# The end of set-up in another order on three engines, and a part of u scaled by GpSimd

## The chip, the cores and the metric

One core of a Trainium2 chip computes the whole problem. The time is device microseconds, the median of several executions. One more execution was taken with the hardware profiler. All times below are from its trace, counted from the first instruction.

## What is computed

The input u has 8 sequences of 1024 positions and 256 channels. The kernel normalises each position over its channels, sends the result through two branches, and adds their product to u:

```python
xn = _layernorm(x, axis=-1)
s = _L0_attn_ref(xn, ...)          # causal filter of 128 taps for each channel, plus xn * D
g = _silu(_L0_ffn_ref(xn, ...))
x = x + s * g
```

`_L0_ffn_ref` is a gated unit, 256 to 704 to 256, whose four operands are rounded to FP4 with one scale for each block of 16 values:

```python
gate = fp4_linear(x, w_gate)
y = fp4_linear(x, w_up)
h = jax.nn.silu(gate) * y
return fp4_linear(h, w_down)
```

The taps of the filter are a real part of a sum of 64 complex exponentials for each channel.

## The kernel before

The 8192 positions are 64 tiles of 128. The gated unit takes two tiles in a step, 32 steps in all (NP). The filter needs the normalised input as fp16 high and low parts in the buffer `xh`, with 16 groups of four tiles.

**Set-up** (to about 91 us) makes the filter's taps `kt`, the statistics of all tiles, and the rounded and transposed weights. Near its end it already treats the first pairs of tiles: `x_norm(p)` on ScalarE (L665) normalises pair p, `x_first` and `x_second` on VectorE (scales at L897 to L902, `inverse` at L930, rounding at L944 and L949) round it, `x_parts` (L957) writes the fp16 parts, `x_transpose` (L1313) and `x_copy` (L672) turn them. `gate_up(m)` (18 matmuls at L1325) makes gate and up of tile m, `silu_gate(m)` (L682) takes SiLU of the gate half, and `h_mult` (L973) multiplies.

**A step** of VectorE first takes the largest of each block (L911, wide TENSOR_REDUCE of 120 blocks), then scales (L914, L918, L922), `inverse` (L930), `h_mult`, rounding (L944 in two pieces, each behind a `square` of ScalarE at L697, then L949), `h_parts` (L981), `x_parts`, and the second `h_mult`. GpSimd makes the tables of scales (`tables`, L515 to L533) between L918 and `h_parts`; VectorE waits for them on `tb_p`. In this order `h_mult` of the next tile opens the way for the next gate_up on TensorE (`h_v`).

**The groups of u** are a third line of work. `a_scale(g)` on ScalarE (L649, four activations of 128x256, normalised with `rs_c` and `nm_c`) is done in place in `gbuf`; `a_high(g)` (L659) writes the fp16 high part; `a_low(g)` on GpSimd (L538) the low part. Each of steps 0 to 7 does the high and low parts of two groups. In steps 4 to 7 a step scales one group (the even one); the odd groups above 5 are the extra ones: before, group 7 in set-up, 9 and 11 in step 1, and 13 and 15 in step 2, all by ScalarE. From step 8 (`S_CONV`) TensorE adds the filter's matmuls (L1358, L1362) to each step, and GpSimd multiplies the branches.

**Order.** Each engine runs the program written for it in line, and they meet in counting semaphores. Nothing is rearranged by a scheduler: what is written first runs first. The taps are scaled on ScalarE (L856, L858: `kt`, `kh`), GpSimd subtracts (`kl`, L587), and SyncE then stores the filter in DRAM (16 DMAs) in step 2 of its own list, between a load of x and a copy of the input to the output. The first `load_t` of the filter is in step 8. Loads of x (L404) wait for `x_r`, which VectorE counts at each L949.

## Time and profile before

| | us |
|---|---|
| median of 3 runs | 572.89 (572.12 to 573.24) |
| the profiled execution | 570.88 |
| its span, first to last instruction | 568.8 |
| VectorE busy | 530.7 (93%) |
| TensorE busy | 477.2 (84%) |
| ScalarE busy | 409.2 (72%) |
| GpSimd busy | 212.0 (37%) |

The busy shares are means over three stretches: set-up to some 91 us, steps 0 to 7 without the filter to some 204 us, and steps 8 to 31 with it. The mean granted clock of TensorE was 0.979. In a timeline a row is one instruction or several of the same kind in a line, with the engine's idle time ahead of it and who ended it in square brackets.

### The profile page before, as it was taken

The numbers are of one execution on the slowest core, as the hardware profiler recorded it, in microseconds if no ns is written. First come the engines' busy times: TensorE is split into PE (matmuls) and PEld (weight loads), VectorE is DVE, ScalarE is ACT, GpSimd is POOL, SyncE is SP. The second block draws the span as 40 slices with busy tenths as digits, with TensorE's granted clock in tenths as the row PEclk, the third lists the DMA queues.
The fourth block names the chain that finished last, engine by engine and source line by source line (L and its number), as shares of the span: only waits on it lengthen the run. The fifth ranks groups of instructions, "written<-read, shape, count | busy, mean of one in ns | idle before, by whom it ended". The sixth has DMA issues, their size and how long they took to land.

```text
span 568.8 us, 13319 instructions
## 1 busy us (share of the span) xinstructions
PE 477.2 (84%) x4981; PEld 332.1 (58%) x4981; DVE 530.7 (93%) x685; ACT 409.2 (72%) x583; POOL 212.0 (37%) x316
## 2 busy tenths in 40 slices
PE   0003474777999999999999999999999999999996
PEld 0000342344555567777777777777777777776675
DVE  6999975898999999999999999999999999999987
ACT  6949758799999976666666666667676666666554
POOL 1499601444555551111111111123233333237770
PEclk9999869889999999999999999999999999999999
DMA  5990002242222135353535353535444353526998
GB/s 162 350 314 1 1 19 93 92 103 94 92 93 94 56 93 165 96 146 100 148 94 167 94 167 93 165 97 145 117 125 135 114 149 112 150 75 124 191 175 177
DMA packets 101954, 70.80 MB, mean 124 GB/s; under 512 B 8864, under 2 KB 101536, under 8 KB 101792
## 3 DMA queue, kind: packets, MB, share of 16 engines
q1 hardware_dynamic: 94624, 62.73, 37.5%
q0 software_dynamic: 7280, 7.34, 8.5%
q8 instruction: 39, 0.64, 0.5%
q14 instruction: 11, 0.09, 0.1%
HBM read 61.28 MB, written 16.12 MB: 136 GB/s over the span
## 4 chain that ended last, share of the span: by engine, by line
PE 63%; DVE 25%; issue 7%; ACT 4%; DMA 0%; SPq 0%; DVEq 0%; ACTq 0%
PE ps L1325 32%; PE ps L1343 10%; PE ps L1345 5%; PE ps L1334 5%; PE ps L1358 4%; PE ps L1362 4%; DVE work L1033 4%; DVE work L949 3%; DVE work L944 3%; DVE work L973 2%; DVE sm L911 2%; PE ps L1313 2%; DVE xh L1011 1%; DVE xh L1001 1%; DVE work L981 1%
## 5 line engine op out<-in xcount | busy, mean ns | idle before, releaser
L1325 PE MATMUL ps<-wgu,work 128*128 128x512 f16 (+1 forms) x1152 | 243.8, 367 | 21.6 <-DVE work L973 20.8
L1325 PEld LDWEIGHTS ps<-wgu,work 128*128 128x128 f16 x1152 | 110.1, 99 | 132.9 <-issue 20.4
L682 ACT ACTIVATE work<-ps,con 128x704 f32<-128x704 f32 x64 | 54.2, 847 | 95.4 <-PE ps L1325 95.4
L1343 PE MATMUL ps<-wdh,work 128*128 128x256 f16 x704 | 87.2, 272 | 0.3 <-ACT work L677 0.2
L677 ACT COPY work<-ps 128x1408 f16<-128x1408 f16 x64 | 84.8, 1325 | 1.6 <-PE ps L1334 1.6
L944 DVE SCALAR_TENSOR_TENSOR work<-work 128x960 f32<-128x960 bf16 (+2 forms) x67 | 72.0, 1112 | 5.0 <-ACT work L697 5.0
L548 POOL TENSOR_TENSOR gbuf<-gbuf,xh 128x256 f32<-128x256 f32 (+1 forms) x42 | 37.8, 929 | 94.0 <-DVE work L957 86.7
L930 DVE TENSOR_TENSOR work<-work,ps 128x960 f32<-128x960 f32 (+2 forms) x67 | 71.5, 1105 | 1.2
L949 DVE SCALAR_TENSOR_TENSOR work<-work 128x1920 f16<-128x1920 bf16 (+3 forms) x36 | 69.7, 1936 | 1.2
L1343 PEld LDWEIGHTS ps<-wdh,work 128*128 128x128 f16 x704 | 65.2, 98 | 7.6 <-ACT work L677 0.4
L911 DVE TENSOR_REDUCE sm<-work 128x120 f32<-128x1920 f32 (+2 forms) x33 | 68.0, 2059 | 1.3
L697 ACT ACTIVATE work<-work 128x960 bf16<-128x960 f32 (+2 forms) x67 | 61.7, 960 | 5.6 <-DVE work L930 5.0
L973 DVE TENSOR_TENSOR work<-work,ps 128x704 f32<-128x704 f32 x64 | 56.4, 881 | 9.0 <-ACT work L682 8.8
L981 DVE TENSOR_TENSOR work<-work,sm 128x1408 f16<-128x1408 f16 (+1 forms) x66 | 54.4, 866 | 5.6 <-DVE work L949 4.2
L515 POOL TENSOR_SCALAR sm<-sm 128x2 int32<-128x2 int32 x32 | 7.6, 239 | 137.6 <-DVE sm L918 137.6
L538 POOL TENSOR_TENSOR xh<-gbuf,xh 128x1024 f16<-128x1024 f32 x16 | 38.8, 2445 | 49.4 <-ACT xh L659 39.4
L686 ACT ACTIVATE gbuf<-ps,sm 128x256 f32 (+1 forms) x64 | 30.2, 473 | 33.0 <-PE ps L1345 32.9
L1334 PE MATMUL ps<-id,work 128*128 128x128 f16 x704 | 49.9, 219 | 3.7 <-DVE work L981 3.6
L1345 PE MATMUL ps<-wdl,work 128*128 128x256 f16 x384 | 52.4, 273 | 0.0
L1358 PE MATMUL ps<-xh,work 128*128 128x64 f16 x768 | 50.3, 192 | 0.0
L1334 PEld LDWEIGHTS ps<-id,work 128*128 128x128 f16 x704 | 43.2, 98 | 11.9 <-DVE work L981 6.0
L1362 PE MATMUL ps<-xh,work 128*128 128x56 f16 x768 | 50.1, 191 | 0.0
(155 smaller groups left out, 682.7 us busy)
## 6 DMA issues: line engine op xcount, KB each, us to landing
work<-kpad SPq DMA_DIRECT2D x64, 512.0 KB, 3.8
gbuf<-u_rev SPq DMA_DIRECT2D x4, 2048.0 KB, 17.9
work<-L_attn_u SPq DMA_DIRECT2D x32, 256.0 KB, 2.9
out<-gbuf POOLq DMA_DIRECT2D x7, 1024.0 KB, 11.5
work<-L_attn_u SPq DMA_DIRECT2D x1, 1024.0 KB, 5.3
out<-gbuf SPq DMA_DIRECT2D x3, 256.0 KB, 2.2
work<-L_ffn_w_down SPq DMA_DIRECT2D x1, 704.0 KB, 7.7
work<-L_ffn_w_gate SPq DMA_DIRECT2D x1, 640.0 KB, 4.6
```

The costliest lines, as they stand in the source:

```text
L677: nc.scalar.copy(hT[par], src).then_inc(hT_a, 1)
L911: own.mark(V.tensor_reduce(bm[:, cols], by_blk[pp][:, cols], AX_X, ALU.max, apply_absolute_value=True))
L930: V.tensor_tensor(v, v, sc, ALU.mult).then_inc(v_v, 1)
L944: own.mark(V.scalar_tensor_tensor(v, d_bf[:, c], C0, v, ALU.add, ALU.subtract))
L949: return V.scalar_tensor_tensor(r_f16[:, c], d_bf[:, c], C0, by_blk[pp][:, c], ALU.add, ALU.subtract)
L973: V.tensor_tensor(vb[par][:, I * t:I * t + I], sg, p_gu[:, I:2 * I], ALU.mult).then_inc(h_v, 1)
L1325: last = T.matmul(p_gu[:, a:b], xT[par][:, t, c, :], wgu[:, part, c % 2, a:b], start=(n == 0), stop=(n == len(todo) - 1))
L1334: last = T.transpose(dst[:, c, :], hilo[par][:, t, c * P:c * P + P], id16[:])
L1343: T.matmul(dst, hT[t][:, c, :], wdh[:, c, :], start=(c == 0), stop=False)
L1345: last = T.matmul(dst, hT[t][:, c, :], wdl[:, c, :], start=False, stop=(c == RT - 1))
L1358: T.matmul(dst, tpl[half][:, 2 * c + tp, 0:P], col[:, xp, :], start=(n == 0), stop=False)
L1362: last = T.matmul(dst1, tpl[half][:, 2 * c + tp, P:2 * P], before, start=False, stop=(n == 2))
```

## The change

The core of the diff:

```diff
@@ GpSimd, end of set-up
-            pool.wait_ge(k_split, 2)
-            nc.gpsimd.tensor_tensor(kl, kt, kh, ALU.subtract).then_inc(k_split, 1)
+            for n, g in enumerate((7, 9, 11)):
+                pool.wait_ge(nm_ok, 2 if n == 0 else 4)
+                if n == 1:
+                    pool.wait_ge(k_free, 1)
+                for t in range(4 * g, 4 * g + 4):
+                    ins = nc.gpsimd.tensor_scalar(gbuf[:, t, :], gbuf[:, t, :], rs_c[:, t:t + 1], nm_c[:, t:t + 1],
+                                                  ALU.mult, ALU.add)
+                ins.then_inc(a_xp, 1)
@@ GpSimd, steps
                 tables(it, it < NP - 2, it >= 1)
+                if it == 1:
+                    pool.wait_ge(k_split, 2)
+                    nc.gpsimd.tensor_tensor(kl, kt, kh, ALU.subtract).then_inc(k_split, 1)
@@ ScalarE
+            input_scales(1)
+            x_norm(2, 0)
+            norm_scales(1)
+            a_scale(13)
             square(-1, 0, True, False, 0)
             act.wait_ge(w_lo, 3)
             act.wait_ge(w_h, 4)
             silu_gate(0)
-            input_scales(1)
-            norm_scales(1)
             weights_out(range(8, 11))
-            x_norm(2, 0)
-            a_scale(7)
+            a_scale(15, 0, 2)
+            square(0, 1, True, False, 0)
+            x_norm(3, 1)
+            silu_gate(1)
+            x_copy(1, 1)
             weights_out(range(11, 13))
+            a_high(0, 2)
+            a_high(1, 2)
+            act.wait_ge(a_xp, 3)
             act.wait_ge(k_sc, 1)
             nc.scalar.activation(kt, kt, ACT.Copy, scale=mxs).then_inc(k_split, 1)
             act.wait_ge(k_split, 1)
             nc.scalar.copy(kh, kt).then_inc(k_split, 1)
-            x_copy(1, 1)
-            for it in range(PEEL):
-                step(it, it % 2, True, it >= 1, True, True, it >= 1, it >= 2, a2=True, td1=it >= 3, first=it >= 1,
-                     more=(None, 9, 13, None)[it])
-                if it in (1, 2):
-                    a_scale(it * 4 + 7)
+            for it in range(1, PEEL):
+                step(it, it % 2, True, True, True, True, True, it >= 2, a2=True, td1=it >= 3, late=it == 1,
+                     more=15 if it == 3 else None)
@@ VectorE
             x_first(1)
+            x_scales()
+            largest(0, 1, True, False)
             largest_of_rows(k_row1, 1, k_one, p_row1)
-            x_scales()
+            h_mult(0, 0, 0)
             x_second(1)
-            h_mult(0, 0, 0)
             x_parts(1, 1)
+            scales(0, True, False)
+            inverse(1, True, False)
@@ TensorE
+            reverse(1)
             pe.wait_ge(w_ca, 8)
             gate_up(0, 0, 0, 1)
-            reverse(1)
+            pe.wait_ge(k_max, 1)
+            T.transpose(p_row1[0:1, :], mxi[:, 3:4], id32).then_inc(k_row1, 1)
...
             gate_up(1, 1, 0, None)
+            pe.wait_ge(con_ok, 1)
+            x_transpose(1, 1)
             pe.wait_ge(w_ca, 9)
             transposed_down(3)
             pe.wait_ge(w_ca, 10)
             transposed_down(4)
-            pe.wait_ge(con_ok, 1)
-            x_transpose(1, 1)
-            pe.wait_ge(w_ca, 13)
```

Step 0 is no longer a step of its own: its pieces are written into set-up on ScalarE and VectorE. VectorE's function `scales_and_largest` is split into `largest` and `scales`. In step 1 `a_scale(2)` of ScalarE comes after `x_norm(4)` (`late`), and step 3 does the second half of group 15 (`more`). The number of groups that `a_high` waits for is adapted. Line numbers of the changed kernel are higher: by 1 in GpSimd's first part, by 10 or 11 in most of ScalarE, by 15 to 22 on VectorE, by 26 to 31 on TensorE.

VectorE before, from the end of `x_first(1)` to the inverse of step 0 (L936, L938 are x_scales; L1039, L1041 largest_of_rows; L1075 to L1163 the powers of the filter's largest):

```order
L930 TENSOR_TENSOR work<-work,ps 128x512
L1039 TENSOR_REDUCE ps<-ps 1x1
L1041 COPY work<-ps 1x128
L936 TENSOR_SCALAR sm<-ps 128x64
L938 SCALAR_TENSOR_TENSOR sm<-ps,sm 128x64
L944 SCALAR_TENSOR_TENSOR work<-work 128x512
L949 SCALAR_TENSOR_TENSOR work<-work 128x512
L973 TENSOR_TENSOR work<-work,ps 128x704
L957 TENSOR_TENSOR work<-work,sm 128x2x256 x2
L1075 TENSOR_SCALAR ps<-ps 128x1
L1077 TENSOR_SCALAR ps<-ps 128x1
L1080 RECIPROCAL ps<-ps 128x1
```
VectorE now, the same stretch (L955, L957 are x_scales; L1058, L1060 largest_of_rows; L992 is h_mult; L976 x_parts):

```order
L955 TENSOR_SCALAR sm<-ps 128x64
L957 SCALAR_TENSOR_TENSOR sm<-ps,sm 128x64
L926 TENSOR_REDUCE sm<-work 128x32
L1058 TENSOR_REDUCE ps<-ps 1x1
L1060 COPY work<-ps 1x128
L992 TENSOR_TENSOR work<-work,ps 128x704
L963 SCALAR_TENSOR_TENSOR work<-work 128x512
L968 SCALAR_TENSOR_TENSOR work<-work 128x512
L976 TENSOR_TENSOR work<-work,sm 128x2x256 x2
L933 SCALAR_TENSOR_TENSOR sm<-sm,ps 128x32
L941 RECIPROCAL ps<-sm 128x32
L949 TENSOR_TENSOR work<-work,ps 128x512
```
The largest, the scales and the inverse of step 0 now stand ahead of the powers, and `h_mult` stands ahead of the rounding.

ScalarE before, from `silu_gate(0)` (L697 ahead of it is square(-1)) to `silu_gate(1)`; L649 is the scaling of group 7, L856 and L858 are the taps:

```order
L665 ACTIVATE work<-work,nmr,rstd 128x256 x2
L649 ACTIVATE gbuf<-gbuf,sm 128x256 x4
L812 COPY wdl<-ps 128x1024
L812 COPY wdl<-ps 128x512
L856 ACTIVATE work<-work 128x256
L858 CAST work<-work 128x256
L672 COPY work<-ps 128x1024
L697 ACTIVATE work<-work 128x512
L665 ACTIVATE work<-work,nmr,rstd 128x256 x2
L659 ACTIVATE xh<-gbuf 128x4x128x2
L682 ACTIVATE work<-ps,con 128x704
```
ScalarE now, from square(-1) (L708) to the taps (L874, L876); L659 is half of group 15, L693 are the two SiLU, L670 both high parts:

```order
L822 COPY wdh<-ps 128x1024 x2
L822 COPY wdh<-ps 128x768
L659 ACTIVATE gbuf<-gbuf,sm 128x256 x2
L708 ACTIVATE work<-work 128x512
L676 ACTIVATE work<-work,nmr,rstd 128x256 x2
L693 ACTIVATE work<-ps,con 128x704
L683 COPY work<-ps 128x1024
L822 COPY wdl<-ps 128x1024
L822 COPY wdl<-ps 128x512
L670 ACTIVATE xh<-gbuf 128x4x128x2 x2
L874 ACTIVATE work<-work 128x256
```
The square of step 0 (L708) and `silu_gate(1)` now stand ahead of the last two copies of weights, the taps behind the high parts of groups 0 and 1.

GpSimd before, from the memset that ends its work on the weights to the tables of step 1:

```order
L585 MEMSET xh 128x2x64
L587 TENSOR_TENSOR work<-work 128x256
L517 TENSOR_SCALAR sm<-sm 128x32
L528 CAST sm<-sm 128x64
L530 TENSOR_TENSOR sm<-sm 128x64
L538 TENSOR_TENSOR xh<-gbuf,xh 128x4x128x2 x2
L515 TENSOR_SCALAR sm<-sm 128x2
```
GpSimd now, the same stretch and the tables of step 1:

```order
L586 MEMSET xh 128x2x64
L592 TENSOR_SCALAR gbuf<-gbuf,sm 128x256 x12
L518 TENSOR_SCALAR sm<-sm 128x32
L529 CAST sm<-sm 128x64
L531 TENSOR_TENSOR sm<-sm 128x64
L539 TENSOR_TENSOR xh<-gbuf,xh 128x4x128x2 x2
L516 TENSOR_SCALAR sm<-sm 128x2
```
The subtraction of the taps (L587) has gone behind the tables of step 1, and twelve scalings of `gbuf` stand in its place.

## Rows read from the trace of the kernel before

**Rows 1.** Busy tenths of VectorE in 40 slices of the span (the page).

```profile
DVE  6999975898999999999999999999999999999987
```

**Rows 2.** Timeline, VectorE, end of set-up: start us, us, engine line, [idle before <-releaser].

```profile
85.97 0.29 DVE L1039 TENSOR_REDUCE ps<-ps 1x1 f32<-1x128 f32 x1 [3.30 <-PE ps L1409]
...
91.74 0.69 DVE L930 TENSOR_TENSOR work<-work,ps 128x512 f32<-128x512 f32 x1
...
97.18 0.69 DVE L944 SCALAR_TENSOR_TENSOR work<-work 128x512 f32<-128x512 bf16 x1 [4.75 <-ACT work L697]
...
100.83 2.15 DVE L911 TENSOR_REDUCE sm<-work 128x120 f32<-128x1920 f32 x1
```

**Rows 3.** Timeline, VectorE, steps 1 to 5.

```profile
107.58 0.89 DVE L973 TENSOR_TENSOR work<-work,ps 128x704 f32<-128x704 f32 x1 [0.93 <-ACT work L682]
...
116.24 2.15 DVE L911 TENSOR_REDUCE sm<-work 128x120 f32<-128x1920 f32 x1
...
130.78 2.15 DVE L911 TENSOR_REDUCE sm<-work 128x120 f32<-128x1920 f32 x1
...
138.14 0.89 DVE L973 TENSOR_TENSOR work<-work,ps 128x704 f32<-128x704 f32 x1 [1.54 <-ACT work L682]
...
146.74 2.15 DVE L911 TENSOR_REDUCE sm<-work 128x120 f32<-128x1920 f32 x1
...
155.52 2.16 DVE L949 SCALAR_TENSOR_TENSOR work<-work 128x1920 f16<-128x1920 bf16 x1
...
161.08 2.15 DVE L911 TENSOR_REDUCE sm<-work 128x120 f32<-128x1920 f32 x1
```

**Rows 4.** Timeline, ScalarE, end of set-up and one later step.

```profile
82.77 0.63 ACT L697 ACTIVATE work<-work 128x512 bf16<-128x512 f32 x1 [4.16 <-DVE work L930]
...
93.36 1.50 ACT L812 COPY wdl<-ps 128x1024 f16<-128x1024 f16 x2 [2.32 <-PE ps L1300]
...
98.03 1.07 ACT L659 ACTIVATE xh<-gbuf 128x1024 f16<-128x1024 f32 x1
...
157.18 0.85 ACT L682 ACTIVATE work<-ps,con 128x704 f32<-128x704 f32 x1 [1.34 <-PE ps L1325]
```

**Rows 5.** Timeline, TensorE, gate_up(1), gate_up(2) and gate_up(4).

```profile
89.14 3.74 PE L1325 MATMUL ps<-wgu,work 128*128 128x512 f16 x18 [2.29 <-DVE work L973]
...
100.88 5.78 PE L1325 MATMUL ps<-wgu,work 128*128 128x512 f16 x18 [6.88 <-DVE work L973]
...
116.28 4.92 PE L1325 MATMUL ps<-wgu,work 128*128 128x512 f16 x18 [0.70 <-DVE work L973]
```

**Rows 6.** Windows: stretch, busy us of each engine, granted clock (PEclk), DMA share, GB/s.

```profile
core 0: us, PE busy (x) PEld busy (x) DVE busy (x) ACT busy (x) POOL busy (x), PEclk, DMA share, GB/s
...
102.00:104.00 2.00, 2.00 (x6) 0.73 (x5) 1.93 (x4) 0.76 (x2) 2.00 (x2) 0.50 0.11 33
```

**Rows 7.** Timeline, GpSimd, tables of step 0 and the low parts of groups 0, 1.

```profile
95.78 0.67 POOL L587 TENSOR_TENSOR work<-work 128x256 f16<-128x256 f32 x1 [29.47 <-ACT work L858]
96.53 0.30 POOL L517 TENSOR_SCALAR sm<-sm 128x32 f32<-128x32 f32 x1
...
97.22 0.81 POOL L530 TENSOR_TENSOR sm<-sm 128x64 f16<-128x64 f32 x1
99.63 4.83 POOL L538 TENSOR_TENSOR xh<-gbuf,xh 128x1024 f16<-128x1024 f32 x2 [1.60 <-DVE work L957]
```

**Rows 8.** DMA issues of the page: loads of x, count, size, median us to landing.

```profile
work<-L_attn_u SPq DMA_DIRECT2D x32, 256.0 KB, 2.9
```

**Rows 9.** Timeline, GpSimd, small operations in steps 1 and 4 and in the tail.

```profile
106.86 0.23 POOL L533 TENSOR_SCALAR sm<-sm 128x2 int32<-128x2 int32 x1
...
153.35 1.14 POOL L533 TENSOR_SCALAR sm<-sm 128x2 int32<-128x2 int32 x1
...
554.70 0.52 POOL L530 TENSOR_TENSOR sm<-sm 128x176 f16<-128x176 f32 x1
```

**Rows 10.** Timeline, VectorE, beside the operations of the group above.

```profile
153.26 2.22 DVE L944 SCALAR_TENSOR_TENSOR work<-work 128x960 f32<-128x960 bf16 x2
...
554.75 1.22 DVE L944 SCALAR_TENSOR_TENSOR work<-work 128x704 f32<-128x704 bf16 x1 [0.24 <-ACT work L697]
```

More of the change, by code:

```diff
@@ L644, in _, with a_scale @@
         def _(act):
[L645 to L647 removed]
+            def a_scale(g, t0=0, t1=4):
+                for t in range(t0, t1):
                     tile = gbuf[:, bass.ds(g * 4 + t, 1), :].rearrange("p o h -> p (o h)")
@@ L710, in y_copy, with step @@
                                      scale=con[:, C_CONV:C_CONV + 1]).then_inc(cv_e, 1)
-            def step(it, par, x, xt, xn, gu, ch, td, a2=False, cv=0, c0=None, td1=True, first=True, more=None):
+            def step(it, par, x, xt, xn, gu, ch, td, a2=False, cv=0, c0=None, td1=True, late=False, more=None):
                 if td:
                     h_copy(it * 2 - 4, 0)
-                if a2 and first:
+                if a2 and not late:
                     a_scale(it * 2)
-                if gu and first:
+                if gu:
                     silu_gate(it * 2)
@@ L733, in step @@
                 if a2:
-                    scaled = (2, 6, 10)[it] if isinstance(it, int) and it < 3 else it + (NT // 8 + 1)
-                    if not first:
-                        a_high(it * 2, scaled)
+                    scaled = it + (5 if isinstance(it, int) and it < 3 else 6)
+                if late:
+                    a_scale(it * 2)
                 if more is not None:
-                    a_scale(more)
+                    a_scale(more, 2)
                 if gu:
@@ L1163, in _, with step @@
             V.tensor_scalar(mxs, minv[:, 3:4], XS, None, ALU.mult).then_inc(k_sc, 1)
-            def step(it, par, x, gu, ch, first=True):
+            round_a(0, 1, 0, XH)
+            last = round_b(1, XH, own.n)
+            dve.wait_ge(tb_p, 1)
+            last.then_inc(x_r, 1)
+            x_parts(2, 0)
+            h_mult(1, 1, 0)
+            def step(it, par, x, gu, ch):
                 pp = 1 - par
                 cols, parted = columns(x, ch), pieces(x, ch)
-                scales_and_largest(it, pp, x, ch)
+                largest(it, pp, x, ch)
+                scales(it, x, ch)
                 inverse(pp, x, ch)
-                if gu and first:
+                if gu:
                     h_mult(it * 2, 0, par)
```

24 lines of the change are left out of this document (12 added, 12 removed).

## The prediction, made before the changed kernel was run

> **What bounds the kernel now.** I read the busy tenths first: VectorE is at 9 nearly everywhere and falls in the slices around 80 to 100 us alone, the end of set-up [rows 1]. From step 8 on TensorE leads and no order of set-up reaches it, so a change here is worth what it shortens between about 60 us and the start of a regular step, and that is handed on unchanged to the end. The measure is the start of the wide TENSOR_REDUCE (L911), which opens a step on VectorE: step 1 opens at 100.83 [rows 2], steps 2, 3, 4, 5 at 116.24, 130.78, 146.74 and 161.08 [rows 3]. So steps 1 to 4 last 15.41, 14.54, 15.96 and 14.34 us; 14.33 is what VectorE's own work takes.
>
> Next come the idle times. Before step 1 VectorE waits 3.30 us for TensorE's row transpose (L1039 at 85.97) and 4.75 us for ScalarE's square (L944 at 97.18), though that square's input was finished at 92.43 [rows 2]. The reason is the order of ScalarE: it idled 4.16 us at 78.6 to 82.8, and later five pieces of work stand ahead of the square, the first of them held by transposes that TensorE does after gate_up(1) [rows 4]. In step 1 VectorE loses 0.93 (gate_up(2) takes 5.78 us after a 6.88 us pause, mostly at a granted clock of 0.50, the lower level of 1.2 GHz; gate_up(1) took 3.74) [rows 3, 5, 6]; in step 3 it loses 1.54 [rows 3] behind group scalings of ScalarE, whose order has two of them ahead of that SiLU.
>
> **The set-up's end, part by part.** Up to 82.67 us (x_first(1) done) nothing in VectorE's order changes. I walk it on with the old durations and spacings: x_scales 0.5, largest 0.7, largest_of_rows 0.6 (its transpose now follows gate_up(0) directly and is ready near 83.4), h_mult(0) 0.9 to 85.4, x_second and x_parts to 87.7, scales, reciprocal and inverse 1.3 to 89.0 (as 91.13 to 92.43 before [rows 2]), powers 0.8, square(0)'s two roundings 1.4, x_parts 1.0, h_mult(1) 0.9. Step 1 opens at 93.1 instead of 100.83: 7.7 us gained. It needs the others in time.
> - ScalarE: input_scales, x_norm(2), norm_scales and a_scale(13) take 4.0 us and fit in the old idle time of 4.16. After square(0) at 89.1 the starts follow at 89.7 (x_norm(3)), 90.7 (silu_gate(1), due at 92.2), 91.4, 92.3 and 93.7 (a_high(0)); ahead of silu_gate(2), at 97.0, all is served. Group 15's first half (1.0) lies in a gap at 86.8. The load for x_norm(3) leaves at 86.8 and lands 2.9 later [rows 8]: just in time.
> - TensorE: gate_up(1) starts at 85.4, not 89.14, and pauses before gate_up(2) (93.1) for under 2 us, not 6.88; I take the full clock, 3.74. The longest pause before 89.14 was 2.29 and the clock held [rows 5].
> - GpSimd: 12 TENSOR_SCALAR of 128x256. No row shows one. The nearest are 0.67 for a TENSOR_TENSOR of 256 columns and 0.30 for a TENSOR_SCALAR of 32 [rows 7]. Bounds: 0.30 and, at the rate of the 64-column row of 0.81, 3.2 us; I take 0.67, same width. Group 7 runs 66.3 to 69.0; groups 9 and 11 start at 78.9 and end at 84.3, before the tables of step 0 (due 88.5).
>
> **A collision on SBUF.** VectorE instructions with two operands in SBUF and GpSimd get in each other's way. GpSimd's L533, 0.23 us undisturbed, takes 1.14 us when it starts just behind L944, and ends as the first of its two pieces ends [rows 9, 10]; the 64-column L530 stretches to 0.81 behind the L944 at 97.18 [rows 7, 2]. In the tail it is VectorE: L944 takes 1.22 us for 704 columns, where 960 take 1.11, when GpSimd's L530 was there first [rows 9, 10]. The Trainium skill, "SBUF — State Buffer", section "SBUF: two separate sides", says the same: the pair of ports that the two engines share is locked for a whole instruction, and the loser blocks; these rows agree. By a price of the skill's "GPSIMD Engine Reference", section 3.1 (1.8 cycles of 1.2 GHz for each element in a tight loop), the scaling would be 0.38 us, and the sum would be better by some 0.2.
>
> Two places follow. (a) Group 7 may run into the subtraction of the weights' low part near 69, and groups 9 and 11 meet the small addition of D near 80: between 0 and 0.7 us each, I take 0.5 together. Step 1 opens at 93.6, **7.2 gained**. (b) In step 1 a_low waits for a_high(0), which ends 1.7 us after the step opens. Before, the pair started 1.2 ahead of the opening [rows 2, 7]. Its 4.83 us now end 6.5 us into the step, just where L944 starts (153.26 against 146.74), and the tables' six small operations (2.5 us alone) stand beside L944 and L949, which last until 10.9 into the step [rows 3, 10]. If each instruction of VectorE lets one through, three are left at its end; 1.6 us pass until tb_p lets h_parts go. Bounds: 0 (GpSimd not hindered) and 2.5. Step 1 takes 15.9, **0.5 lost** against 15.41, though the 1.08 of the cold matmul are back.
>
> **Steps 2 and 3.** If step 1 stalls there, TensorE pauses for some 4 us instead of 2.5 between gate_up(3) and the transposes. In step 2 before, gate_up(4) took 4.92 after the shorter pauses; after the long pause 5.78 was paid and VectorE waited 0.93 [rows 5, 3]. Step 2: 15.3, **0.8 lost**; bounds +0.2 and -0.9. Step 3 loses two group scalings ahead of its h_mult, since groups 9 and 13 are gone from the steps and 11, 15 too; the half group left (1.0) fits in the 1.34 us gap before the second SiLU of a step [rows 4]. It takes 14.33, **1.6 gained**. The filter's last subtraction moves behind the tables of step 1 on GpSimd, near 107; SyncE's sixteen stores of it have 11 us of issue ahead of copy_input(2) and the load of x 6, and these keep their place to the step. First use is at step 8: no cost.
>
> **Sum.** 7.2 - 0.5 - 0.8 + 1.6 = 7.5 us. The profiled execution, 570.88 (span 568.8 and 2.1 around it), would be 563.4. It lies 2.0 below the median of 572.89, and the gain is the same for both: **565.4** by the median.
>
> **The rivals.**
> 1. No collision in step 1: GpSimd ends in time or its small operations slip through. Then 7.5 + 1.1 + 0.1 + 1.6 = 10.3, **562.6**. For it: only one operation in a row was seen to be held, and 0.5 us of earlier a_low frees two more. Against: the rows above, and that a_high(0) stands behind four pieces on ScalarE.
> 2. The tight places slip as well: the load of x 3 lands a microsecond later, with silu_gate(1) and a_high(0) behind it. That is 1 us at the opening of step 1 and up to 1 more at the tables: 5.5 gained, **567.4**. Its slack is 0.5 us.
> 3. Slower: the scaling on GpSimd is dear. The tables of step 0 stand behind the 8 operations of groups 9 and 11 and VectorE's x_parts(2) behind the tables. Up to 1.4 us each it is hidden; from 2.65 us each the whole gain is gone; at the upper bound of 3.2 the tables end near 106 and step 1 opens at 108.3, 7.5 late, against 2.7 won in steps 1 and 3: **577.7**. Against it: wide GpSimd rows run at 2.4 (L538) and 2.6 ns (L587) a column, and the 64-column row of 0.81 was a held one [rows 7].
> 4. It does not reach the end: something fixed in time, the filter in DRAM or the input copies, opens step 8, and **572.9** stays. Against it: the filter was in place before 130 us and step 8 opens at 204.
>
> **Numbers.** Chances: forecast 0.50, rival 1 0.27, rival 2 0.14, rival 3 0.05, rival 4 0.04. The forecast's own range is 564.2 to 566.7. The whole range reaches to rivals 1 and 2: 562.0 to 567.7. Some 0.2% (1.1 us) is what a measurement of this kernel can tell from no change. Faster 0.91, same 0.04, slower 0.05.
>
> **What would show it.** In the changed profile: the wide TENSOR_REDUCE of step 1 at 93 to 94; no wait over 1 us on VectorE between 83 and that; gate_up(1) in 3.7 us from 85.4; twelve TENSOR_SCALAR near 0.67. For the collision: some of the tables' small operations at 1 to 2 us and a wait of 1 to 2 us on VectorE for GpSimd before the first wide L981; for step 2 a gate_up(4) of over 5 us; then steps of 14.33. It is wrong if GpSimd's scaling lasts over 1.4 us, if step 1 opens after 95, or if steps 4 to 7 differ from 14.33.

## The result, and the profile after

| | before | changed |
|---|---|---|
| median of the runs timed together, us | 572.5 (570.53 to 573.24, 4 runs) | 562.81 (562.41 to 563.28, 4 runs) |
| ratio, 95% interval | | 0.9832 (0.9808 to 0.9856) |
| profiled execution, us | 570.88 | 563.28 |
| its span, us (granted TensorE clock) | 568.8 (0.979) | 561.5 (0.977) |
| step 1 opens, us | 100.83 | 92.93 |
| steps 1, 2, 3, 4, 5, us | 15.41, 14.54, 15.96, 14.34, 14.32 | 16.72, 14.92, 14.23, 14.39, 14.71 |

The change gains 9.7 us by the medians, 1.7%, and 7.6 us between the two profiled executions. The sum of the prediction was 7.5 us, and for the profiled execution it fits (563.4 forecast, 563.28 measured). The median was forecast as 565.4; the measured 562.81 lies 2.6 below that, outside the forecast's own range (564.2 to 566.7) and inside the whole one (562.0 to 567.7). So two things need explaining: how good the single terms are behind a sum that fits, and where the other 2 us come from. Of these, 1.6 are on the side of before (its profiled execution 570.88, its median 572.5) and 0.5 on the side of the changed kernel (563.28 and 562.81).

The page of the changed kernel: the line of totals, and VectorE's busy tenths over the span, as [rows 1].

```profile
PE 478.2 (85%) x4981; PEld 332.7 (59%) x4981; DVE 531.4 (95%) x685; ACT 404.7 (72%) x571; POOL 220.2 (39%) x328
...
DVE  6999999899999999999999999999999999999987
```

The dip at 80 to 100 us is gone; one slice at 8 is left, the end of step 1. The timeline of VectorE there, against [rows 2, 3] (start us, us, engine, line, operation, idle time before it and who ended it; L911 of before is L926 now, L944 is L963, L949 is L968, L973 is L992, L981 is L1000, L1039 is L1058):

```profile
84.04 0.28 DVE L1058 TENSOR_REDUCE ps<-ps 1x1 f32<-1x128 f32 x1
...
89.76 0.69 DVE L963 SCALAR_TENSOR_TENSOR work<-work 128x512 f32<-128x512 bf16 x1
...
92.93 2.15 DVE L926 TENSOR_REDUCE sm<-work 128x120 f32<-128x1920 f32 x1
...
99.46 2.58 DVE L963 SCALAR_TENSOR_TENSOR work<-work 128x960 f32<-128x960 bf16 x2
102.07 2.16 DVE L968 SCALAR_TENSOR_TENSOR work<-work 128x1920 f16<-128x1920 bf16 x1
105.90 2.17 DVE L1000 TENSOR_TENSOR work<-work,sm 128x1408 f16<-128x1408 f16 x2 [1.68 <-POOL sm L531]
...
109.65 2.15 DVE L926 TENSOR_REDUCE sm<-work 128x120 f32<-128x1920 f32 x1
```

Both waits of set-up, 3.30 and 4.75 us in [rows 2], are gone, and the two rows on which they stood (now 84.04 and 89.76) have no idle time before them. Step 1 opens 7.9 us earlier. A new wait stands in step 1: 1.68 us for L531, the last operation of GpSimd's tables. GpSimd in the same stretch, after its twelve scaling operations (L592, in two runs of 4 and 8); [rows 7, 9] are its rows of before:

```profile
66.27 2.17 POOL L592 TENSOR_SCALAR gbuf<-gbuf,sm 128x256 f32<-128x256 f32 x4
79.43 4.35 POOL L592 TENSOR_SCALAR gbuf<-gbuf,sm 128x256 f32<-128x256 f32 x8 [10.99 <-ACT sm L806]
...
95.10 4.85 POOL L539 TENSOR_TENSOR xh<-gbuf,xh 128x1024 f16<-128x1024 f32 x2 [6.12 <-ACT xh L670]
99.91 1.14 POOL L516 TENSOR_SCALAR sm<-sm 128x2 int32<-128x2 int32 x1
101.13 1.07 POOL L518 TENSOR_SCALAR sm<-sm 128x32 f32<-128x32 f32 x1
102.28 2.00 POOL L521 TENSOR_SCALAR sm<-sm 128x2 int32<-128x2 int32 x1
104.36 0.34 POOL L524 TENSOR_TENSOR sm<-sm 128x88 f32<-128x88 f32 x1
104.77 0.38 POOL L529 CAST sm<-sm 128x240 bf16<-128x240 f32 x1
105.23 0.64 POOL L531 TENSOR_TENSOR sm<-sm 128x240 f16<-128x240 f32 x1
...
106.02 1.30 POOL L635 TENSOR_TENSOR work<-work 128x256 f16<-128x256 f32 x1
```

VectorE's two pairs, taken one instruction at a time, and the second of GpSimd's two L539:

```profile
99.46 1.51 DVE L963 SCALAR_TENSOR_TENSOR work<-work 128x960 f32<-128x960 bf16 x1
100.89 1.14 DVE L963 SCALAR_TENSOR_TENSOR work<-work 128x960 f32<-128x960 bf16 x1
...
106.71 1.36 DVE L1000 TENSOR_TENSOR work<-work,sm 128x1408 f16<-128x1408 f16 x1
```

```profile
97.50 2.46 POOL L539 TENSOR_TENSOR xh<-gbuf,xh 128x1024 f16<-128x1024 f32 x1
```

Read GpSimd's ends against VectorE's rows. The first small operation ends at 101.05, just behind the first L963 (100.97); the second at 102.20, just behind the second (102.04); the third at 104.28, just behind L968 (104.23). Each instruction of VectorE let one through. Three were left, and they took another 1.5 us, in which VectorE stood still.

VectorE loses time in two instructions only. The first L963 starts at 99.46, while L539 still runs (until 99.95), and takes 1.51 instead of 1.15. The second L1000 starts at 106.71, while the difference of the taps, L635, still runs (until 107.32), and takes 1.36 instead of 0.88. In both it loses what was left of GpSimd's operation, less some 0.14 us.

TensorE's gate_up(0) to gate_up(4) (18 matmuls each; L1325 of before is L1356), against [rows 5]:

```profile
77.84 5.87 PE L1356 MATMUL ps<-wgu,work 128*128 128x512 f16 x18 [0.22 <-ACT wgu L822]
85.66 3.74 PE L1356 MATMUL ps<-wgu,work 128*128 128x512 f16 x18 [0.31 <-DVE work L992]
92.97 3.73 PE L1356 MATMUL ps<-wgu,work 128*128 128x512 f16 x18 [1.94 <-DVE work L992]
99.60 5.24 PE L1356 MATMUL ps<-wgu,work 128*128 128x512 f16 x18 [2.46 <-DVE work L992]
109.69 5.30 PE L1356 MATMUL ps<-wgu,work 128*128 128x512 f16 x18 [0.77 <-DVE work L992]
```

The pause of 6.88 us of [rows 5] is 1.94 now, and gate_up(2) takes 3.73 instead of 5.78. Behind set-up the slow ones are gate_up(3) and gate_up(4). The windows of that stretch (columns as in [rows 6]; the last but two is the granted clock) show the lower of the two levels, 1.2 GHz, for both:

```profile
100.00:102.00 2.00, 2.00 (x7) 0.83 (x6) 2.00 (x2) 2.00 (x4) 1.92 (x2) 0.50 0.00 0
110.00:112.00 2.00, 2.00 (x7) 0.77 (x6) 1.97 (x2) 2.00 (x5) 2.00 (x2) 0.50 0.21 19
```

### The profile page after: what moved, and what is told of

Read it like the earlier page. It is cut to its first block, busy times and chain, and to the rows that moved or that the text cites. A ratio compares the mean times of both kernels' runs of the same rounds, so it can differ in the third digit from the quotient of the medians.

```text
span 561.5 us, 13319 instructions
## 1 busy us (share of the span) xinstructions
PE 478.2 (85%) x4981; PEld 332.7 (59%) x4981; DVE 531.4 (95%) x685; ACT 404.7 (72%) x571; POOL 220.2 (39%) x328
## 4 chain that ended last, share of the span: by engine, by line
PE 62%; DVE 26%; issue 6%; ACT 3%; POOL 2%; DMA 0%; SPq 0%; DVEq 0%; ACTq 0%; POOLq 0%
PE ps L1356 32%; PE ps L1374 10%; PE ps L1376 5%; PE ps L1365 5%; PE ps L1389 4%; PE ps L1393 4%; DVE work L968 3%; DVE work L1052 3%; DVE work L963 2%; DVE sm L926 2%; DVE work L992 2%; PE ps L1344 2%; DVE xh L1030 2%; DVE work L1000 1%; DVE work L976 1%
## 5 line engine op out<-in xcount | busy, mean ns | idle before, releaser
L1356 PE MATMUL ps<-wgu,work 128*128 128x512 f16 (+1 forms) x1152 | 243.9, 367 | 15.2 <-DVE work L992 15.0
L1356 PEld LDWEIGHTS ps<-wgu,work 128*128 128x128 f16 x1152 | 110.2, 99 | 126.6 <-issue 14.0
L693 ACT ACTIVATE work<-ps,con 128x704 f32<-128x704 f32 x64 | 54.3, 848 | 96.4 <-PE ps L1356 96.3
L963 DVE SCALAR_TENSOR_TENSOR work<-work 128x960 f32<-128x960 bf16 (+2 forms) x67 | 72.5, 1119 | 0.3 <-ACT work L708 0.2
L949 DVE TENSOR_TENSOR work<-work,ps 128x960 f32<-128x960 f32 (+2 forms) x67 | 71.4, 1105 | 1.2
L968 DVE SCALAR_TENSOR_TENSOR work<-work 128x1920 f16<-128x1920 bf16 (+3 forms) x36 | 69.7, 1936 | 1.2
L926 DVE TENSOR_REDUCE sm<-work 128x120 f32<-128x1920 f32 (+2 forms) x33 | 68.0, 2059 | 1.3
L708 ACT ACTIVATE work<-work 128x960 bf16<-128x960 f32 (+2 forms) x67 | 61.9, 960 | 3.4 <-DVE work L949 2.8
L1000 DVE TENSOR_TENSOR work<-work,sm 128x1408 f16<-128x1408 f16 (+1 forms) x66 | 54.9, 873 | 8.6 <-DVE work L968 5.0
L992 DVE TENSOR_TENSOR work<-work,ps 128x704 f32<-128x704 f32 x64 | 56.4, 881 | 5.6 <-ACT work L693 5.5
L539 POOL TENSOR_TENSOR xh<-gbuf,xh 128x1024 f16<-128x1024 f32 x16 | 38.8, 2445 | 47.1 <-ACT xh L670 26.6
L697 ACT ACTIVATE gbuf<-ps,sm 128x256 f32 (+1 forms) x64 | 30.3, 474 | 32.9 <-PE ps L1376 32.8
L1365 PE MATMUL ps<-id,work 128*128 128x128 f16 x704 | 49.8, 219 | 4.5 <-DVE work L1000 4.3
L1365 PEld LDWEIGHTS ps<-id,work 128*128 128x128 f16 x704 | 43.2, 98 | 12.8 <-DVE work L1000 7.0
```

Source lines behind the costliest of these rows:

```text
L926: own.mark(V.tensor_reduce(bm[:, cols], by_blk[pp][:, cols], AX_X, ALU.max, apply_absolute_value=True))
L949: V.tensor_tensor(v, v, sc, ALU.mult).then_inc(v_v, 1)
L963: own.mark(V.scalar_tensor_tensor(v, d_bf[:, c], C0, v, ALU.add, ALU.subtract))
L968: return V.scalar_tensor_tensor(r_f16[:, c], d_bf[:, c], C0, by_blk[pp][:, c], ALU.add, ALU.subtract)
L992: V.tensor_tensor(vb[par][:, I * t:I * t + I], sg, p_gu[:, I:2 * I], ALU.mult).then_inc(h_v, 1)
L1356: last = T.matmul(p_gu[:, a:b], xT[par][:, t, c, :], wgu[:, part, c % 2, a:b], start=(n == 0), stop=(n == len(todo) - 1))
```

## The experiments

Four questions are asked: does the order or the scaling bring the gain; is the loss of step 1 the collision on SBUF; is the loss of step 2 the clock; and why do the medians differ by 2 us more than the traces. Each kernel's step openings and lengths are read from the starts of the wide TENSOR_REDUCE. The kernels were timed on three chips, each beside the kernel of before: the first four rows on one (before 572.55), the next four on another (before 573.29), the last two on a third (before 572.23). The ratios compare across them; differences of medians are given within one chip unless the text says otherwise.

| kernel | median us (runs) | ratio to before (95%) | step 1 opens | steps 1, 2, 3, 4 |
|---|---|---|---|---|
| before (steps of its second trace) | 572.55 (13) | 1 | 100.8 | 15.26, 14.46, 15.93, 14.35 |
| scale_only | 573.24 (10) | 1.0003 (0.998 to 1.0025) | 103.0 | 15.75, 14.72, 15.94, 14.36 |
| order_only | 565.16 (4) | 0.9871 (0.9839 to 0.9904) | 92.6 | 16.75, 14.30, 14.73, 15.36 |
| low_cut | 561.23 (4) | 0.9793 (0.9761 to 0.9826) | 93.2 | 14.96, 14.30, 14.23, 14.39 |
| changed, again | 562.73 (5) | 0.9825 (0.9804 to 0.9845) | 92.4 | 16.72, 14.77, 14.26, 14.36 |
| early_high | 561.47 (5) | 0.98 (0.9781 to 0.982) | 92.5 | 15.38, 15.02, 14.23, 14.39 |
| warm | 563.53 (5) | 0.9835 (0.9816 to 0.9853) | 93.1 | 16.82, 14.96, 14.23, 14.41 |
| taps_late | 564.45 (4) | 0.9849 (0.9825 to 0.9873) | 92.4 | 16.25, 15.02, 14.55, 16.37 |
| before_warm | 571.43 (10) | 0.9984 (0.9967 to 1.0) | 100.9 | 14.30, 16.31, 17.24, 14.35 |
| early_warm | 562.44 (5) | 0.9822 (0.9795 to 0.9848) | 92.9 | 15.30, 14.30, 15.62, 14.35 |

**The kernel of before, profiled again.**

> The kernel before, unchanged, profiled a second time. The forecast took the gain by the trace and by the median for the same, but they came out as 7.6 and 9.7 us. Theory A (the profiled execution of before was a quick one, and executions of one kernel differ in TensorE's granted clock in set-up): this trace has a span that differs from 568.8 by 0.5 to 3 us, and the difference stands ahead of step 4 (146.74 in the first trace), in the duration of some matmuls of set-up or of a gate_up of steps 1 and 2. Rival B (the changed kernel gains after step 4 in most executions, not in the profiled one): the step openings agree with the first trace within 0.3 us, and the span is within 0.5 us of 568.8.

Measured: 570.65 us, with a span of 568.6 and every opening within 0.25 us of the first trace. The other executions of before on that chip reached from 570.5 to 574.8, median 572.55, and their spans go with the mean granted clock: 568.5 to 568.7 at 0.979, 570.2 to 572.5 at 0.973, 572.8 at 0.970. This was another short one, so it shows the spread and not yet its place.

**The scaling on GpSimd without the new order.** The order of before on all engines; GpSimd takes groups 7, 9 and 11, ScalarE keeps 13 and 15:

```diff
@@ GpSimd, end of set-up
+            for n, g in enumerate((7, 9, 11)):
...
+                for t in range(4 * g, 4 * g + 4):
+                    ins = nc.gpsimd.tensor_scalar(gbuf[:, t, :], gbuf[:, t, :], rs_c[:, t:t + 1], nm_c[:, t:t + 1],
+                                                  ALU.mult, ALU.add)
...
@@ ScalarE
-            a_scale(7)
+            act.wait_ge(a_xp, 3)
...
-                     more=(None, 9, 13, None)[it])
-                if it in (1, 2):
+                     more=(None, None, 13, None)[it])
+                if it == 2:
                     a_scale(it * 4 + 7)
```

> The kernel before in its old order; only the scaling of groups 7, 9 and 11 is GpSimd's, and ScalarE does 13 and 15 in step 2 as it did. By the forecast's account the parts are separate: step 1 still opens near 100.8, step 1 keeps its 15.4, and of the 1.54 us that VectorE waited in step 3 most goes, since ScalarE has 4.1 us less to do in step 1; but 13 and 15 are still in step 2. Expected gain 0.5 to 1.6 us over before (571.0 to 572.0 by a median of 572.5). Rival (ScalarE's scaling was what held set-up): step 1 opens 2 us earlier, and the gain is 3 us or more. Second rival (GpSimd's twelve operations hinder VectorE by themselves): slower than before by up to 0.7.

Measured: nothing gained, 1.0003. Step 3 kept its 15.94: the scalings taken from ScalarE were those of set-up and step 1, and in step 2 its order is as before, two of them (from 134.78 and 137.97) right ahead of the SiLU for which VectorE waits 1.52 us in step 3. In set-up GpSimd's run of eight collided with VectorE, and both lost. The timelines of VectorE (L953 and L958 are the two roundings of one tile; [rows 2] has the first at 0.69) and of GpSimd:

```profile
86.94 0.81 DVE L953 SCALAR_TENSOR_TENSOR work<-work 128x512 f32<-128x512 bf16 x1
87.79 0.93 DVE L958 SCALAR_TENSOR_TENSOR work<-work 128x512 f16<-128x512 bf16 x1
...
99.35 0.69 DVE L953 SCALAR_TENSOR_TENSOR work<-work 128x512 f32<-128x512 bf16 x1 [6.38 <-ACT work L706]
```

```profile
84.53 5.16 POOL L592 TENSOR_SCALAR gbuf<-gbuf,sm 128x256 f32<-128x256 f32 x8 [16.06 <-ACT sm L805]
```

Eight operations took 5.16 us here, and 4.35 where the changed kernel has them; one by one, six keep 0.55 to 0.56 and the two beside the roundings take 0.98. This trace also has gate_up(1) at 5.42 us, and with it a wait of 6.38 where [rows 2] has 4.75. So in the old order this scaling gains nothing. Whether it would with groups 13 and 15 moved as well was not tried.

**The new order without the scaling on GpSimd.** Groups 7, 9 and 11 go back to ScalarE, one in each of steps 1, 2 and 3:

```diff
+                if isinstance(it, int) and it in (1, 2, 3) and a2:
+                    a_scale(it * 2 + 5)
```

> The changed kernel with the scaling of groups 7, 9 and 11 taken from GpSimd and given back to ScalarE, one group in each of steps 1, 2 and 3 ahead of the second SiLU; groups 13 and 15 stay as changed. By the forecast's account the opening of step 1 stays at 93 to 94, and the collision on SBUF too. Steps 1 and 2 have 1.2 to 2.8 us of idle time on ScalarE, so they hide most of a group's 2.07; step 3 has 1.34 and gets 3.1 us of scaling, so VectorE loses 1 to 2 us there. Expected 564.0 to 566.0. Rival (GpSimd's scaling is what makes the new order work at all): step 1 opens later than 95, and 567 or more.

Measured: 565.16, as forecast. Step 3 takes 14.73 and step 4 15.36, against 14.23 and 14.39 in the changed kernel. The expectation had 1 to 2 us in step 3, in a wait of VectorE for ScalarE. The sum is right and the way is another: VectorE waits for no SiLU in step 3 and 0.18 us in step 4. It is the collision again. With more to do, ScalarE gives the high parts later, GpSimd's tables come later, and VectorE's roundings meet them in both steps (2.22 and 2.16 undisturbed):

```profile
130.14 2.40 DVE L956 SCALAR_TENSOR_TENSOR work<-work 128x960 f32<-128x960 bf16 x2
132.58 2.48 DVE L961 SCALAR_TENSOR_TENSOR work<-work 128x1920 f16<-128x1920 bf16 x1
...
145.24 2.86 DVE L956 SCALAR_TENSOR_TENSOR work<-work 128x960 f32<-128x960 bf16 x2
```

So the order alone brings 7.4 us of the 9.7 by the medians, and the scaling, which gains nothing in the old order, brings 2.2 to 2.4 more behind it (two chips). The traces show 1.5 of that, in steps 3 and 4. This trace gets 0.5 to 0.6 back in step 2, which takes 14.30, and it was this kernel's shortest execution, 563.92; where the rest lies was not traced. It also has all of step 1's loss, the wait of 1.68 and 16.75 us, without GpSimd's scaling: that loss belongs to the order.

**The low parts of groups 0 and 1 set to zero.** This kernel leaves part of the computation out: GpSimd writes zeros in place of two differences of 1024 columns, which take 1.91 us instead of 4.85.

```diff
+                if g < 2:
+                    nc.gpsimd.memset(x_part(1, g), 0.0).then_inc(a_lp, 1)
+                    return
```

> The changed kernel, in which GpSimd fills the low parts of groups 0 and 1 with zeros instead of subtracting (that part of the result is left out), so its tables of step 1 start earlier. If the stretched small operations and the wait of 1.7 us on VectorE come from the collision with L963 and L968, the tables run at their 2.5 us between about 96.5 and 99.5, step 1 takes 14.33 instead of 16.72, and step 2 falls from 14.92 to 14.3 to 14.6, since TensorE pauses less: 2.6 to 3.0 us gained over the changed kernel, 559.8 to 560.3. Rival (the small operations are slow for another reason, or step 2's loss has nothing to do with step 1): the tables stay near 5 us, or step 2 keeps 14.9.

Measured: 561.23, 1.6 us below the changed kernel's 562.81 (timed on another chip; by the ratios to before, 0.9793 and 0.9832, it is 2.2). GpSimd's timeline:

```profile
95.32 1.91 POOL L540 MEMSET xh<- 128x1024 f16 x2 [6.10 <-ACT xh L673]
97.20 0.22 POOL L516 TENSOR_SCALAR sm<-sm 128x2 int32<-128x2 int32 x1
...
99.02 0.64 POOL L531 TENSOR_TENSOR sm<-sm 128x240 f16<-128x240 f32 x1
```

The same six operations that took 5.96 us now take 2.46, since VectorE's instructions with two operands in SBUF start only at 100.27. Step 1 is 1.76 us shorter, the wait for the tables is gone, and step 2 takes 14.30. The theory of the collision stands. The time expected was a microsecond lower still: gate_up(2) took 5.25 us here although it followed the same pause of 1.94 us after which it took 3.73 in the changed kernel, and VectorE waited 0.39 for it, so that step 1 would be 2.1 us shorter without the collision but for this. The same pause met the fall of the clock in one execution and not in the other.

**The changed kernel again, in five rounds.**

> The changed kernel, unchanged, timed and profiled a second time beside the kernels of this call. Theory (the old order has gate_up(1) on VectorE's path, the new one does not): executions of the kernel before spread over 570.5 to 574.8 us, as gate_up(1) runs at 3.74 or 5.42 us and gate_up(2) likewise; those of the changed kernel stay within 562.2 to 563.6 with a median near 562.8, and step 1 opens within 0.6 us of 92.93 whatever gate_up(1) takes. Rival (the spread is of the chip, not of the order): the changed kernel spreads over 4 us as well.

Measured: 562.73 (562.33 to 563.68); before beside it 573.29 (571.8 to 574.94, 9 runs). Step 1 took 16.72 again. So the changed kernel spreads over 1.35 us and that of before over 3.1 here and over 4.3 on the two other chips. The gain by medians, 10.6 here, is again above that by traces.

**The high parts earlier.** TensorE makes the transposes for groups 3 and 4 of the down weights ahead of gate_up(1), so that ScalarE copies all of them out together and reaches a_high(0) sooner; the halves of group 15 go to steps 1 and 3:

```diff
             transposed_down(2)
-            gate_up(1, 1, 0, None)
-            pe.wait_ge(con_ok, 1)
-            x_transpose(1, 1)
             pe.wait_ge(w_ca, 9)
...
             transposed_down(4)
+            gate_up(1, 1, 0, None)
+            pe.wait_ge(con_ok, 1)
+            x_transpose(1, 1)
```

> The changed kernel with the last two transposes of the down weights ahead of gate_up(1) on TensorE and their copies ahead of the square of step 0 on ScalarE; the first half of group 15 goes to step 1. The high parts of groups 0 and 1 then start 1.4 us sooner and GpSimd's tables of step 1 near 98.3 instead of 99.9. By the collision theory three of their six operations are done before VectorE's L963, the tables end near 102 and the wait of 1.68 us goes: step 1 takes 14.4 to 14.9, step 2 14.3 to 14.9, 560.4 to 561.6. Price: gate_up(1) starts 1 us later (86.7); at its short duration that is hidden, at 5.4 us it would hold silu_gate(1) and cost 1 us. Rival (GpSimd's operations are held from L963 on whatever their order, or the subtractions themselves are what is held): the wait stays over 1 us, 562.3 or more.

Measured: **561.47 (561.25 to 562.36)**, 1.3 us below the changed kernel on the same chip, and the fastest kernel here that computes everything. GpSimd's and VectorE's timelines in step 1:

```profile
93.12 4.85 POOL L539 TENSOR_TENSOR xh<-gbuf,xh 128x1024 f16<-128x1024 f32 x2 [4.59 <-ACT xh L670]
...
99.30 1.19 POOL L529 CAST sm<-sm 128x240 bf16<-128x240 f32 x1
100.57 1.43 POOL L531 TENSOR_TENSOR sm<-sm 128x240 f16<-128x240 f32 x1
101.97 2.13 POOL L534 TENSOR_SCALAR sm<-sm 128x2 int32<-128x2 int32 x1
```

```profile
99.01 2.48 DVE L961 SCALAR_TENSOR_TENSOR work<-work 128x960 f32<-128x960 bf16 x2
101.53 2.48 DVE L966 SCALAR_TENSOR_TENSOR work<-work 128x1920 f16<-128x1920 bf16 x1
104.10 2.18 DVE L998 TENSOR_TENSOR work<-work,sm 128x1408 f16<-128x1408 f16 x2
```

Two microseconds of head start on L539 let four small operations start before VectorE's pair does, and the wait for the tables is gone. What is left is seen in VectorE's own rows: 2.48, 2.48 and 2.18, where undisturbed ones take 2.22, 2.16 and 1.69. That is 1.07 us, all by which step 1's 15.38 exceeds 14.30. Step 1 came out above the expected range for that reason; step 2, at 15.02, lies above its range too, behind a gate_up(4) of 5.40.

**Matmuls to keep TensorE busy in steps 1 to 3.** 32 more matmuls whose results nobody reads, in the places of its pauses:

```diff
+            def stay_busy(count):
+
+                for n in range(count):
+                    T.matmul(ps[:, 3072:3072 + H], id16[:], wgu[:, 0, 0, 0:H], start=True, stop=True)
...
+                if isinstance(it, int) and it in (2, 3):
+                    stay_busy(12 if it == 2 else 6)
...
+                if isinstance(it, int) and it == 1:
+                    stay_busy(8)
...
+            pe.wait_ge(w_ca, 11)
+            stay_busy(6)
```

> The changed kernel with 32 extra matmuls of 256 columns on TensorE, in its pauses of steps 1 to 3, into a bank that nobody reads. Theory (steps 1 and 2 lose because TensorE falls to the lower clock in its pauses): gate_up(3) and gate_up(4), 5.24 and 5.30 us in the first trace, run in 3.74; step 2 takes 14.3 instead of 14.92, step 1 keeps its 16.7 since its loss is the wait for GpSimd; 0.5 to 0.7 us gained, 562.1 to 562.4. Rival (the clock is not what step 2 waits for): gate_up(4) is short and step 2 keeps 14.9, nothing gained or a loss of some tenths from the extra work.

Measured: 563.53, 0.8 above the changed kernel beside it. gate_up(3) took 3.74, as it did in the second trace of the changed kernel without any extra work. gate_up(4) took 5.34: the windows from 109 to 111 and 111 to 113 us have the granted clock at 0.72 and 0.50. This decided nothing about step 2.

**The taps' difference a step later.** GpSimd's L635 moves from behind the tables of step 1 to behind those of step 2:

```diff
-                if it == 1:
+                if it == 2:
```

> The changed kernel with the subtraction of the taps on GpSimd (L635) one step later, behind the tables of step 2. In the changed kernel it stood beside VectorE's first wide L1000 of step 1, whose pair took 2.17 us instead of 1.69. If it is this subtraction that held it, the pair is back at 1.69 in step 1 and step 1 takes 16.2; the filter is stored 15 us later, still 60 us ahead of its first use: 0.3 to 0.5 us gained, 562.3 to 562.5. Rival: the pair of step 1 keeps 2.17 (something else held it), or another two-operand instruction of step 2 takes the same loss, so nothing is gained.

Measured: the pair of L1000 went from 2.17 back to 1.69 and step 1 from 16.72 to 16.25, as expected; the kernel, expected to gain 0.3 to 0.5, is 1.7 us slower. The queue of SyncE shows why (its issues, and ScalarE's next wait):

```profile
115.94 10.36 SPq L442 DMA_DIRECT2D kpad<-work  x16
...
127.00 0.58 SPq L405 DMA_DIRECT2D work<-L_attn_u  x1
```

```profile
134.45 1.09 ACT L676 ACTIVATE work<-work,nmr,rstd 128x256 f32<-128x256 f32 x2 [2.67 <-DMA work<-L_attn_u]
```

The sixteen stores of the filter take 10.36 us to issue. Here they stand in front of a load of x, and ScalarE waits 2.67 us for that load; step 4 takes 16.37. In the changed kernel the same stores stand a step earlier (from 107.35), behind that step's load of x, and nobody waits. The prediction had put their move at no cost, which was right by one step's margin.

**The kernel of before, a third time.**

> The kernel before, unchanged, a third look. Both profiled executions so far were quick ones (span 568.6 and 568.8, mean granted clock 0.979), where most executions of it have 0.973 and a span near 570.6. Theory: if this one is of the longer kind, its trace has gate_up(1) at 5.4 us instead of 3.74, step 1 opens at 102.5 to 103.0 instead of 100.8, and from there all is as before. If it is a quick one it tells nothing more. Rival: a longer execution loses its 2 us somewhere behind step 4.

Measured: 573.15 us, span 571.4 at a granted clock of 0.973; this is the long kind. Its timelines of TensorE and VectorE, against [rows 5, 2]:

```profile
77.64 6.67 PE L1325 MATMUL ps<-wgu,work 128*128 128x512 f16 x18 [0.84 <-ACT wgu L812]
...
90.29 5.42 PE L1325 MATMUL ps<-wgu,work 128*128 128x512 f16 x18 [2.30 <-DVE work L973]
```

```profile
87.12 0.29 DVE L1039 TENSOR_REDUCE ps<-ps 1x1 f32<-1x128 f32 x1 [4.18 <-PE ps L1409]
...
100.01 0.69 DVE L944 SCALAR_TENSOR_TENSOR work<-work 128x512 f32<-128x512 bf16 x1 [6.43 <-ACT work L697]
```

gate_up(0) took 1.1 us longer than in the short executions and gate_up(1) 1.7 longer, behind the same pause of 2.30. The windows from 90 to 92 us, in this trace and in the first one of before, show the granted clock at 0.61 and at 1.00:

```profile
90.00:92.00 2.00, 1.71 (x5) 0.72 (x6) 1.90 (x9) 2.00 (x5) 0.00 (x0) 0.61 1.59 557
```

```profile
90.00:92.00 2.00, 2.00 (x12) 0.98 (x11) 1.83 (x8) 1.04 (x3) 0.00 (x0) 1.00 1.65 627
```

The two waits of VectorE grew by 0.9 and 1.7. Step 1 opens at 103.7, and from there the steps are those of the second trace (15.22, 14.44, 15.93, 14.35). The 2.8 us by which this span exceeds that one's are all lost in set-up. scale_only's trace has the second of the two in the old order as well: gate_up(1) at 5.42 and a wait of 6.38.

**The kernel of before, kept busy ahead of gate_up(1) and gate_up(2).** 16 and 50 more matmuls:

```diff
+            pe.wait_ge(w_ca, 9)
+            stay_busy(16, 2048)
             gate_up(1, 1, 0, None)
...
             pe.wait_ge(w_ca, 13)
+            stay_busy(50, 3072)
             for it in range(1, NP - 1):
```

> The kernel before with 16 extra matmuls of 256 columns on TensorE ahead of gate_up(1) and 50 ahead of gate_up(2), in its pauses of 2.3 and 6.9 us, into banks that nobody reads. Theory (the old order is exposed to TensorE's clock in both places, the new one in neither): gate_up(1) and gate_up(2) take 3.74 in every execution, step 1 opens near 100.8 and takes 14.4; the median falls from 572.5 or 573.3 to 569.4 to 570.2 and the spread to 1.5 us. With that the changed kernel's gain of 9.7 to 10.6 by the median would stand as 7.6 of order and 2 to 3 of exposure. Rival (the spread has another origin): the extra matmuls change the median by less than 1 us and the spread stays over 3 us.

Measured: gate_up(1) 3.74, gate_up(2) 3.73, step 1 14.30 (against 15.2 to 15.4), and a spread of 2.0 us against 4.3 of before beside it. That much is as expected, though gate_up(1) took 3.74 in both short executions of before too. The median is 0.8 below that of before, not 2 to 3, which is what the rival had. Steps 2 and 3 gave the gain back, with 16.31 and 17.24, behind slow groups of TensorE:

```profile
107.56 5.42 PE L1325 MATMUL ps<-wgu,work 128*128 128x512 f16 x18 [2.46 <-DVE work L973]
...
122.88 6.70 PE L1325 MATMUL ps<-wgu,work 128*128 128x512 f16 x18 [2.94 <-DVE work L973]
```

So this kernel does not measure what the clock in set-up costs the median. It trades one slow group for others, and its traced execution was the longest of its ten (572.8).

**early_high, kept busy ahead of gate_up(4).** 24 more matmuls ahead of step 2's transposes.

> The variant with the earlier high parts (561.5 us) and 24 extra matmuls of 256 columns between gate_up(3) and the first transposes of h in step 2, where TensorE pauses for 3.5 us and gate_up(4) then took 5.40. Twelve of them had been too few in the changed kernel: gate_up(4) stayed at 5.34. Theory: with 2.6 of the 3.5 us filled the clock holds, gate_up(4) takes 3.74, step 2 takes 14.3 to 14.5 instead of 15.0, and the median is 560.8 to 561.1. Rival (step 2's loss is not the clock): gate_up(4) is short and step 2 still takes 14.9 or more. Second rival: the clock falls all the same, and the transposes behind the extra work are late: 561.5 to 562.5.

Measured: in step 2 the theory holds. gate_up(4) takes 3.73 and the step 14.30 instead of 15.02. But the next one pays, and more: gate_up(5) 5.42 instead of 3.74, and step 3 15.62 instead of 14.23. The kernel is 1.0 us slower than early_high (medians from two chips).

```profile
108.21 3.73 PE L1354 MATMUL ps<-wgu,work 128*128 128x512 f16 x18 [0.26 <-DVE work L990]
114.84 5.42 PE L1354 MATMUL ps<-wgu,work 128*128 128x512 f16 x18 [2.46 <-DVE work L990]
```

All eight traces with the new order fit one reading of step 2. With gate_up(4) at 3.73, 4.60 or 4.62 the step takes 14.30; above that it grows with it (5.14 and 14.77, 5.30 and 14.92, 5.40 and 15.02). So the group has some 0.95 us of slack over its full-clock time, and then VectorE pays all of the rest.

## Why the prediction was right, and where it was not

- **Set-up.** Forecast 93.6, measured 92.93 and 92.4. The mechanism is the one described: both waits gone, gate_up(1) at 85.66 in 3.74 us, no VectorE wait in the stretch. The forecast was 0.7 to 1.2 late. 0.5 of that was a price for two small collisions of GpSimd that did not show (the twelve operations took 0.54 us each, not the 0.67 of the forecast nor the 0.38 of the estimate beside it, and both runs kept the same rate). The walk itself was long by 0.6 to 0.7: from the end of x_first(1) it has 10.4 us, and the traces 9.8 and 9.7. In the profiled execution x_first(1) ended 0.47 later than before, which hides part of that.
- **Step 1.** The wait was forecast at 1.6 us and measured at 1.68; three operations were left at VectorE's end, as forecast. The step still took 16.72 and not 15.9. The mis-sized term is VectorE's side, 0.84 us that the prediction put at nothing: the pair of L963 takes 2.58, not 2.22, since its first instruction finds L539 still running, and the pair of L1000 2.17, not 1.69, since its second finds the difference of the taps (L635), which the prediction had moved "near 107" without asking what runs there. The prediction had read this side of the collision from its row of the tail and left it out of the sum. low_cut has the pair of L963 at 2.31 without L539, and taps_late that of L1000 at 1.69 without L635. The loss was 1.3 where 0.5 was forecast.
- **Step 2.** Forecast 0.8 lost, 0.4 measured; gate_up(4) took 5.30, over 5 us as forecast. early_warm shows that it is this matmul group: with it at 3.73 the step takes 14.30. The link to step 1 that the prediction made does not hold: order_only stalls in step 1 just as long (1.68) and has gate_up(4) at 4.62 and 14.30, and early_high does not stall for GpSimd and has 5.40 and 15.02. What differs is when the clock falls. In order_only the window from 108 to 110 us has it at 0.50 and that from 112 on at 1.00 again; in the changed kernel that from 108 has 0.87, that from 110 0.50 and that from 112 0.77.
- **Step 3.** Forecast 14.33, measured 14.23: the wait of 1.54 behind ScalarE's scalings is gone.
- **Later.** Step 4 opens 7.94 us earlier (138.80 against 146.74). Step 5 gives 0.4 back (14.71, and 14.67 to 14.71 in all eight traces with the new order, against 14.32). The prediction had named a step 4 to 7 other than 14.33 as a sign of being wrong. In the trace VectorE waits 0.53 us there, at L1000, for TensorE's L1365, and before 0.18 at the same place; why TensorE is later was not tested. The rest reaches the end: the span is 7.3 shorter.
- **The sum.** Against the forecast the terms are off by +0.7 (set-up), -0.8 (step 1), +0.4 (step 2), +0.1 (step 3) and -0.3 (behind step 4, by the two execution times; -0.6 by the spans). That they add up to the profiled execution within 0.1 us is luck.
- **The step that failed** is the last one of the sum: "the gain is the same for both", for the profiled execution and for the median. 570.88 is a short execution of before; its medians are 1.4 to 2.4 longer. before_third shows where a long one loses: gate_up(0) and gate_up(1) meet the lower clock for longer, and in the old order ScalarE and VectorE wait for both (the waits of 3.30 and 4.75 that the change removes). In the new order the pause ahead of gate_up(1) is at most 0.35 us and not 2.3, gate_up(1) took 3.73 or 3.74 in all eight traces, and step 1 opened between 92.4 and 93.2 with gate_up(0) anywhere from 5.15 to 6.10. So the change removes most of that loss, and the spread with it (1.35 us against 3.1 to 4.3). For one long execution this is shown; that the median of before is long for the same reason is an inference, since none near 572.5 was traced in that kernel and before_warm could not settle it. With 572.89 at hand beside 570.88, and the waits known to hang on two matmul groups that run at a varying clock, this could have been asked ahead.
- **The rivals.** No collision (562.6) gives nearly the measured number and is wrong: the collision is there and costs 1.6 us by the medians, 1.8 to 2.1 by the traces. It is the difference between trace and median, of 2.1, that put the time there. (The rival's own sum starts from 7.5 for set-up, where the text has 7.2; with 7.2 it gives 10.0 and 562.9.) The scaling was cheap, and it reached the end; the tight places held.
What stays open: why the fall of the clock meets one pause in one execution and another in the next, what the executions of before near its median lose and where, why step 5 is longer in the new order, and where the last 0.7 to 0.9 us of the scaling's gain (order_only against the changed kernel, by medians) lie.
